# Six norm applications of the joined feed-forward and projection stage: from VectorE to ScalarE, with a bias made by GpSimd

## The reference

```
ln(v) = (v - mean) / sqrt(var + 1e-5)
x = x + attention0(ln(x), ctx)                 # 16 heads of 16
x = x + ffn0(ln(x))                            # activations rounded to 8 bits, weights to -1, 0, 1
x = x + layer1(ln(x), ctx)                     # starts with a second norm with gains (ln1),
                                               # then causal self-attention a1 (16 heads of 32), its
                                               # feed-forward, cross-attention a2, its feed-forward
x = x + moe(ln(x))                             # 8 experts, one chosen for each token

ffn0: q = round(x * 127 / max|x|)              # "front quant", one scale for each token
      h = silu(q @ Wgate) * (q @ Wup)          # 1024 wide
      y = round(h * 127 / max|h|) @ Wdown      # "hidden quant", one scale for each token
```

## Time and profile before

| | us |
|---|---|
| median of 3 runs (range) | 1103.15 (1103.12 to 1103.85) |
| profiled execution, first to last instruction (span) | 1100.8 |
| difference, what lies around the span | 2.35 |
| PE busy | 1034.3 (94%) |
| DVE busy | 535.6 (49%) |
| ACT busy | 465.3 (42%) |
| POOL busy | 268.5 (24%) |

### The profile page before, as it was taken

One profiled execution on the slowest core, in us unless ns is written; L12 is line 12 of the kernel. 1 busy time (PEld: TensorE's weight loads), 2 busy tenths in 40 slices (PEclk: granted clock), 3 DMA queues, 4 the chain that ended last, 5 costly groups with the idle time before them and its releaser, 6 DMA issues.

```text
span 1100.8 us, 20861 instructions
## 1 busy us (share of the span) xinstructions
PE 1034.3 (94%) x8679; PEld 741.0 (67%) x8679; DVE 535.6 (49%) x1293; ACT 465.3 (42%) x715; POOL 268.5 (24%) x409
## 2 busy tenths in 40 slices
PE   7998887999989999999999999999999999999997
PEld 4655544455467777776676475667578658999996
DVE  5567789985257788741531333775332233200000
ACT  6767555675455555552222325554311231122220
POOL 3023201100023334332212110566320102322211
PEclk9999989999999999999999999999999999999999
DMA  8700000000070000000000020000710217755410
GB/s 255 90 2 1 1 1 1 1 1 0 1 153 2 2 3 2 2 1 1 1 1 0 1 96 1 2 2 2 229 39 20 96 42 275 282 190 189 161 51 1
DMA packets 55359, 60.56 MB, mean 55 GB/s; under 512 B 23603, under 2 KB 47071, under 8 KB 55266
## 3 DMA queue, kind: packets, MB, share of 16 engines
q1 hardware_dynamic: 52322, 52.93, 16.3%
q0 software_dynamic: 2944, 6.30, 1.8%
HBM read 54.76 MB, written 7.21 MB: 56 GB/s over the span
## 4 chain that ended last, share of the span: by engine, by line
PE 74%; DVE 18%; ACT 3%; issue 2%; POOL 1%; SPq 1%; DMA 0%; DVEq 0%; ACTq 0%; POOLq 0%
PE ps L1882 15%; PE ps L2182 10%; DVE small L790 9%; PE ps L2324 8%; PE ps L2337 7%; PE ps L1742 6%; PE ps L2006 3%; PE ps L1713 3%; PE ps L2257 3%; PE ps L1795 2%; PE ps L1733 2%; PE ps L1710 2%; PE ps L1651 2%; PE ps L2008 1%; PE ps L1808 1%
## 5 line engine op out<-in xcount | busy, mean ns | idle before, releaser
L790 DVE TENSOR_REDUCE small<-ps 128x4 f32<-128x1024 f32 (+2 forms) x112 | 145.4, 1334 | 96.1 <-PE ps L1713 60.0
L1882 PE MATMUL ps<-r_w,r_k 128*128 128x256 f32 x512 | 113.2, 381 | 2.5 <-ACT r_k L1552 2.5
L2182 PE MATMUL ps<-r_a,r_w 128*128 128x512 f32 x256 | 112.1, 594 | 3.1 <-ACT r_a L1385 3.1
L1882 PEld LDWEIGHTS ps<-r_w,r_k 128*128 128x128 f32 x512 | 96.4, 190 | 18.6 <-issue 4.4
L1795 PE MATMUL ps<-r_a,onesf 128*32 128x256 f32 (+1 forms) x768 | 84.3, 387 | 8.3 <-ACT r_a L1305 8.3
L2182 PEld LDWEIGHTS ps<-r_a,r_w 128*128 128x128 f32 x256 | 48.2, 190 | 60.2 <-issue 56.0
L2324 PE MATMUL ps<-r_a,w_block 128*128 128x128 f32 x736 | 86.4, 275 | 1.0 <-ACT r_a L1613 1.0
L2324 PEld LDWEIGHTS ps<-r_a,w_block 128*128 128x128 f32 x736 | 85.6, 192 | 2.5 <-ACT r_a L1613 1.0
L1552 ACT ACTIVATE r_k<-ps,pvec 128x512 f32<-128x512 f32 x64 | 44.0, 687 | 100.6 <-PE ps L2182 100.6
L1305 ACT ACTIVATE r_a<-ps 120x1024 f32<-120x1024 f32 (+1 forms) x64 | 65.5, 1024 | 43.4 <-PE ps L1749 43.2
L2337 PE MATMUL ps<-w_all,r_a 128*128 x368 | 83.2, 379 | 0.2 <-issue 0.2
(11 more groups left out here) (265 smaller groups left out, 1819.9 us busy)
## 6 DMA issues: line engine op xcount, KB each, us to landing
w_block<-in_L_ffn_W SPq DMA_DIRECT2D x23, 1024.0 KB, 5.9
w_all<-in_L_ffn_W SPq DMA_DIRECT2D x8, 1024.0 KB, 9.5
r_w<-in_L_xattn_a_li_w SPq DMA_DIRECT2D x4, 1024.0 KB, 7.4
x_rows<-x_all SPq DMA_DIRECT2D x4, 512.0 KB, 3.0
x_rows<-r_a SPq DMA_DIRECT2D x4, 512.0 KB, 3.0
x_all<-in_x SPq DMA_DIRECT2D x3, 512.0 KB, 5.9
y_all<-in_L_ffn_w_gate SPq DMA_DIRECT2D x1, 1024.0 KB, 8.7
y_all<-in_L_ffn_w_up SPq DMA_DIRECT2D x1, 1024.0 KB, 11.1
```

The source lines that it names most:

```text
L790: ins_ = dve.tensor_reduce(nm.rearrange("p (j s) -> p j s", j=4)[:, j:j + count, :], src, AX.X, ALU.max, negate=True)
L1882: ins_ = pe.matmul(o[:, t // 2, (t % 2) * D:(t % 2 + 1) * D], src[:, c, t * P:(t + 1) * P], w[:, c, :], start=(c == 0), stop=(c == chunks ...
L2182: ins_ = pe.matmul(o, LI[a]["li2"][:, c, m * P:(m + 1) * P], FT3[:, c, :], start=(c == 0), stop=(c == KC - 1))
```

## The change

GpSimd's `rstd` gets a form `shift=True`: after the power it multiplies the means with the result and subtracts that from zero, so that `small` holds the bias -mean * rstd as well; only then is `rstd_ready` raised. Six of the norms of the stage use it: f of pairs 1, 2, 3 and n of pairs 0, 1, 2. Their application leaves VectorE's stream and enters ScalarE's, as four Identity activations with scale rstd and that bias. f of pair 0 and n of pair 3 stay as they were. VectorE waits for the new semaphore `xhb_ready` ahead of `front_scales(1)`, `(2)` and `(3)`. On ScalarE the six stand here (the order of all else is kept):

- `front_apply(1)` behind `silu(0,0,1)`, ahead of `weights_copy(2)`;
- `second_norm(0)` behind `whole_copy(1,0)`, ahead of `silu(1,2,1)`; `front_apply(2)` behind that `silu`, ahead of `silu(1,3,0)`;
- `front_apply(3)` behind `silu(2,0,1)`, ahead of `whole(1,3)` and `project_copy(0,3)`;
- `second_norm(1)` behind `whole_copy(2,1)`, ahead of `project_copy(0,7)`;
- `second_norm(2)` behind `project_copy(1,8)`, ahead of `whole_copy(3,1)` and `project_copy(1,9)`.

```diff
@@ GpSimd
-                def rstd(tiles=PT_TILES, twice=False):
+                def rstd(tiles=PT_TILES, twice=False, shift=False):
...
+                    if shift:
+                        link(pool.tensor_tensor(sa(at + 72, tiles), ve, neghalf[:, 0:tiles], ALU.pow))
+                        mean = sa(at + 48, 2 * tiles).rearrange("p (t k) -> p t k", k=2)[:, :, 0]
+                        link(pool.tensor_tensor(sa(at + SHIFT, tiles), mean, sa(at + 72, tiles), ALU.mult))
+                        pool.tensor_tensor(sa(at + SHIFT, tiles), zeros[:, 0:tiles], sa(at + SHIFT, tiles), ALU.subtract
+                                           ).then_inc(sem["rstd_ready"], 1)
@@ VectorE
                 gated(0, 0, 0)
-                front_apply(1, kf1)
                 gated(0, 0, 1)
+                dve.wait_ge(sem["xhb_ready"], 1)
                 front_scales(1)
...
                 attended_sum(3)
-                second_norm(0, kn0)
                 gated(1, 2, 1)
-                front_apply(2, kf2)
                 hidden_quant(1, 1)
...
                 gated(2, 0, 1)
-                front_apply(3, kf3)
                 hidden_quant(2, 0)
...
                 hidden_quant(2, 2)
-                second_norm(1, kn1)
                 down_sum(2, 0)
+                dve.wait_ge(sem["xhb_ready"], 3)
...
                 kn2 = normed_stats(2)
-                second_norm(2, kn2)
                 gated(3, 2, 1)
@@ ScalarE
+                def shifted(dst, src, k):
+                    act.wait_ge(sem["rstd_ready"], k + 1)
+                    at = LN_W * (k % 4)
+                    for t in range(PT_TILES):
+                        ins_ = act.activation(dst[:, t, :], src[:, t, :], ACT.Identity, bias=sa(at + SHIFT + t, 1), scale=sa(at + 72 + t, 1))
+                    return ins_
+
+                def front_apply(p, k):
+                    act.wait_ge(sem["n1_ready"], p)
+                    shifted(XHB, X[p], k).then_inc(sem["xhb_ready"], 1)
+
+                def second_norm(p, k):
+                    shifted(XHC, Y[p], k).then_inc(sem["c_xh_ready"], 1)
```

More of the change, by code:

```diff
@@ L67, in build @@
         epst = sb("epst", [P, 8]); neghalf = sb("neghalf", [P, 8])
-        onepe = sb("onepe", [P, 4]); eps2 = sb("eps2", [P, 4])
+        zeros = sb("zeros", [P, 4]); onepe = sb("onepe", [P, 4]); eps2 = sb("eps2", [P, 4])
         eidx = sb("eidx", [P, E])
@@ L216, in build @@
         CTX_STATS, CTX_APPLY = (16, 17, 18, 19), (21, 22, 23, 24)
-        LN_W = 80
+        LN_W, SHIFT = 80, 24
         NMX, RS, AM, SC, SU, SGT, SUT, SD = 320, 336, 352, 356, 360, 364, 372, 380
@@ L306, in build @@
                  "li1_done", "xb_ready", "yb_ready", "xh3_ready", "x3T_done", "ft3_ready", "xhq_ready", "xqT_done", "ftq_ready",
-                 "r_done", "r_ready", "dn_done", "y_ready", "cxh_ready", "cyT_done", "cyT_ready", "d_lid_ready",
+                 "r_done", "r_ready", "dn_done", "y_ready", "cxh_ready", "cyT_done", "cyT_ready", "d_lid_ready", "xhb_ready",
                  "x5_last_stored", "x5h_last_stored", "x5_half", "chosen", "x5_ready", "dn_half", "xh_half", "xT_half", "fq_half", "logits_done", "lg_ready", "x_pre_ready"]
@@ L491, in rstd @@
                         link(pool.tensor_tensor(ve, v, epst[:, 0:tiles], ALU.add))
-                    pool.tensor_tensor(sa(at + 72, tiles), ve, neghalf[:, 0:tiles], ALU.pow).then_inc(sem["rstd_ready"], 1)
+                    if shift:
[4 more added lines that the diff above has]
+                                           ).then_inc(sem["rstd_ready"], 1)
+                    else:
+                        pool.tensor_tensor(sa(at + 72, tiles), ve, neghalf[:, 0:tiles], ALU.pow).then_inc(sem["rstd_ready"], 1)
                 pool.memset(small[:], 0.0)
@@ L499, in _ @@
                 pool.memset(onepe[:], 1.0 + EPS)
+                pool.memset(zeros[:], 0.0)
                 pool.memset(eps2[:], EPS * EPS)
@@ L558, in _ @@
                         pool.tensor_tensor(X[p], X[p], bv("L0_xattn_bo"), ALU.add).then_inc(sem["xbo_ready"], 1)
-                rstd()
-                rstd()
+                rstd(shift=True)
+                rstd(shift=True)
                 rstd(twice=True)
-                rstd()
-                rstd()
+                rstd(shift=True)
+                rstd(shift=True)
                 rstd(twice=True)
-                rstd()
+                rstd(shift=True)
                 rstd(twice=True)
-                rstd()
+                rstd(shift=True)
                 rstd(twice=True)
@@ L992, in _ @@
                 hidden_quant(1, 2)
+                dve.wait_ge(sem["xhb_ready"], 2)
                 front_scales(2)
@@ L1394, in a1_input @@
                                 ).then_inc(sem[f"c_ft{e}_ready"], 1)
+                NORM_OF = {n: NP + 2 + i for i, n in enumerate(("f1", "f2", "o0", "n0", "f3", "o1", "n1", "o2", "n2"))}
+                def shifted(dst, src, k):
[9 more added lines that the diff above has]
+                    shifted(XHC, Y[p], k).then_inc(sem["c_xh_ready"], 1)
                 def project_copy(p, k):
@@ L1407, in _ @@
                 silu(0, 0, 1)
+                front_apply(1, NORM_OF["f1"])
                 weights_copy(2)
@@ L1430, in _ @@
                 whole_copy(1, 0)
+                second_norm(0, NORM_OF["n0"])
                 silu(1, 2, 1)
+                front_apply(2, NORM_OF["f2"])
                 silu(1, 3, 0)
@@ L1445, in _ @@
                 silu(2, 0, 1)
+                front_apply(3, NORM_OF["f3"])
                 whole(1, 3)
@@ L1459, in _ @@
                 whole_copy(2, 1)
+                second_norm(1, NORM_OF["n1"])
                 project_copy(0, 7)
@@ L1491, in _ @@
                 project_copy(1, 8)
+                second_norm(2, NORM_OF["n2"])
                 whole_copy(3, 1)
```

## The result

| | before | after |
|---|---|---|
| median, us (range, runs) | 1103.13 (1102.46 to 1103.85, 4) | 1123.6 (1122.23 to 1123.98, 4) |
| ratio (95% interval) | | 1.0182 (1.017 to 1.0195) |
| span of the profiled execution, us | 1100.8 | 1122.0 |

What follows compares the result with a forecast made beforehand. VectorE leads from 130 to 183 us, VectorE and TensorE are both full to 226, TensorE leads to 271. Onto 1103.15 us the places add 14.65 and the clock 2.35, together 17.0: 1120.2 us, 8-in-10 range 1109.5 to 1125.

Steps and rivals of the forecast that it cites:

- f of pair 1: ScalarE's weight copies, needed by VectorE's gated and TensorE's output(2), start at 142.82 instead of 141.43: +1.3 us.
- n of pair 0 and f of pair 2: ScalarE's a1_input copies end at 188.1, so TensorE's project(0,0) starts there for 186.05: +2.1 us.
- f of pair 3: TensorE's hidden_transposes(1,3), behind whole(1,3), starts 5.57 us late, 3.7 us of it standing still: +3.45 us on top.
- n of pair 1, standing still: TensorE's project(0,9) needs project_copy(0,7), which stands behind this norm on ScalarE: 6.6 us standstill, +6.65 us.
- given back behind it: After the project(0,9) standstill VectorE is early, so TensorE's idle 0.84 us at 224.50 goes: -0.55 us.
- n of pair 2: TensorE's project(1,11) moves +2.8 us behind project_copy(1,9); project(2,0) starts at 261.83 for 260.17: +1.7 us.
- clock, both falls: TensorE slower behind gaps: one full 1.5 us fall after the 6.6 us standstill, half after 3.7 us: +2.35 us.
- The ScalarE price: Four 128x256 activations with scale and bias from tiles take 1.93 us; six sets 11.6 us (7.5 to 16.7).
- The GpSimd tail: Product and subtraction after GpSimd's power cost 0.56 us; norm ready 1.93 us after the statistics end, before 1.4.
- A: Rival: each norm is done before ScalarE's next item is ready, so VectorE's relief pays: 1097.6 us, chance 0.05.
- B: Rival: offsets between the six places overlap instead of adding: slower, 1105.4 to 1112 us, chance 0.12.
- C: Rival: TensorE's clock falls after every new gap, 6.0 us instead of 2.35: 1123.8 us, chance 0.15.

Runs made afterwards that it cites:

- Experiment 4: Kernel before with GpSimd's added product and subtraction for the six norms, VectorE still applying them and ScalarE unchanged: 1105.37 us, ratio 1.0023.
- Experiment 3: Kernel after with unused matmuls on TensorE, 15 ahead of hidden_transposes(1,3) and 30 ahead of project(0,9): 1119.73 us, ratio 1.0143.
- experiment 9: Kernel before with only f of pairs 2 and 3 on ScalarE, placed where its stream idles: 1103.57 us, ratio 1.0003.
- experiment 6: Kernel before with only n of pair 1 on ScalarE, at the change's place: 1113.02 us, ratio 1.0087.
- experiment 7: Kernel before with only f of pairs 1 to 3 on ScalarE, at the change's places: 1110.14 us, ratio 1.0068.
- experiment 8: Kernel before with only n of pairs 0 and 2 on ScalarE, at the change's places: 1107.33 us, ratio 1.004.
- experiment 1: Kernel after with n of pair 1 back on VectorE, the other five norms staying on ScalarE: 1114.95 us, ratio 1.01.
- experiment 5: Kernel after with plain copies, without scale or bias, in place of the 24 activations: 1118.21 us, ratio 1.0133.
- experiment 2: Kernel after with n of pair 1 later on ScalarE, ahead of whole(2,2) instead of project_copy(0,7): 1115.69 us, ratio 1.0118.

## Why the prediction was right

The direction and the mechanism came out as written, and TensorE lost time at each of the places that the prediction names; the size of the first was right, the others were too small, and what was to be given back too large. The measured 1123.6 lies in the range from 1109.5 to 1125, but over the band of 1112 to 1122.5 to which I had given 0.60. Each term as TensorE's offset between the two profiles shows it:

| step | forecast, us | measured, us |
|---|---|---|
| start of the stage, before any norm | 0 | 0.4 |
| f of pair 1 | 1.3 | 1.3 |
| n of pair 0 and f of pair 2 | 2.1 | 2.35 |
| f of pair 3 | 3.45 | 3.6 |
| n of pair 1, standing still | 6.65 | 7.5 |
| given back behind it | -0.55 | -0.4 |
| n of pair 2 | 1.7 | 2.0 |
| clock, both falls | 2.35 | 3.4 |
| DMA wait at 941 us | 0 | 0.9 |
| sum | 17.0 | 21.1 (21.2 by the spans) |

The lines on the start and on the DMA wait are no effects of the change; without them the profile shows 19.8 us. The forecast for the clock has a small slip: one fall of 1.5 us and a half one make 2.3, and 2.35 was carried.

**The ScalarE price.** I took 1.93 us for a set; it is 2.06 to 2.08, each activation 583 to 600 ns. Six sets put 0.8 us on the sum. This is the term where I set the nearer row, which is 240 columns wide, above the better price. By the figures of the Trainium skill (ScalarE: Activation LUTs, What ACT_TABLE_LOAD costs) the estimates were 585 ns and 2.06 us a set, and the rows agree with the set to 0.02 us.

**The GpSimd tail.** 0.56 us was right five times of six (0.20 us each, 0.08 between). At n of pair 1 the last subtraction took 0.73 us, so the norm was ready half a microsecond later than I had it, at the place where every bit is paid. That is the main part of 7.5 for 6.65. Experiment 4 shows that at n of pair 2 the tail is paid even when VectorE applies the norm.

**The clock.** The step that was mis-sized most. I counted one fall of 1.5 us behind the long gap and half of one behind the short. Both fell in full: 3.56 us for 1.89 at the first (1.4 us net), and 7.51 for 5.4 at the second (2.0 us), where the rows show 0.50 up to 234 us and 0.74 in the two microseconds behind. Experiment 3 filled both gaps and took 3.9 us off. With two falls of 1.7 in the sum the forecast would have been 1121.2.

**What would show it.** Four of the seven signs are there as promised: 3.71 us before `hidden_transposes(1,3)`; 2.67 us at `project(1,11)`; ScalarE idle on GpSimd before f of pair 3 and n of pairs 0, 1 and 2; the clock at 0.50 behind the longest gap. Two are there in another size: the 24 activations take 0.59 us each for 0.55, and the gap before `project(0,9)` is 7.30 us for 6 to 7. The last was off: VectorE is busy 7.0 us less, not 8.3. Its groups of normalizing instructions did lose 8.2 us (28.5 to 20.3); the rest of the difference isn't in any one group.

**The rivals.** A, VectorE's relief pays: no place of the change has it, and experiment 9, with two norms that hold nothing up, shows none either. B, overlap: its 1105.4 to 1112 is out by the result, and experiments 6 to 8 show the places adding up. C, a fall of the clock behind every gap, 1123.8: the time that came is C's, but by luck: the falls cost 3.4 us and not C's 6.0, and what is missing there is in the other terms, which were short. The clock fell behind 3.71 and 7.30 us; behind the 2.67 us gap the four matmuls took 1.98 us, full speed. In other profiles the gap at this place does bring a fall: the same four take 2.98 us in experiment 1, 3.54 in experiment 3 and, behind a gap of only 1.93 us, 3.42 in experiment 5. The Trainium skill (TensorE: Matmul & The Clock Gate, HAM oscillation), by which idle gaps put the array back at half rate each time anew, was right for the two longer gaps and in some executions for the third; it deserved more weight than I gave it.

Of the ten ranges expected of the experiments, those of 4 and 9 missed. What stays open: where the 0.2 to 0.9 us at the start of the stage come from; why the same gap brings a fall of the clock in one execution and not in another, which may also be behind the slower executions among the four of experiments 1 and 3; and whether the 1 us by which the whole is less than its parts is more than chance.

## What to carry to other kernels

A busy share says that an engine has time, not when. Before work moves to an engine with room, look up what stands behind it in that engine's stream, when its input is ready, and who waits for the next item: here one norm, ready 5.4 us after ScalarE came to it, stopped projections that never used it, and four copies further down it cost 8 us less. Where TensorE stands still for microseconds, add the slower work behind the gap to the gap itself.

## What the runs showed of the hardware

- GpSimd's 128x4 subtraction took 0.20 us at five of the six norms. At n of pair 1 it took 0.73, and ended 0.06 us after a VectorE instruction that it ran beside. The two engines' rows of the kernel after:

```profile
227.40 0.73 POOL L496 TENSOR_TENSOR small<-zeros,small 128x4 f32<-128x4 f32 x1
```

```profile
227.33 0.74 DVE L924 TENSOR_SCALAR r_a<-r_a,small 128x1024 f32<-128x1024 f32 x1
```

  The subtraction took 0.73 or 0.74 us there in every profile that has it at n of pair 1 (experiments 2 to 6), and at no other norm. The product just before it ran its 0.20 us beside two VectorE instructions of one column. The Trainium skill (SBUF — State Buffer, SBUF: two separate sides) says that the two engines share a port pair that one of them holds for a whole instruction; these rows agree.
- An activation with scale and bias from a tile took 586 to 588 ns for 256 float32 columns, a plain copy of the same 404.
- Work that is thrown away can pay: 45 unused matmuls in the kernel after saved 3.9 us by the medians, 43 in the kernel before 1.9 us. The granted clock behind the filled gaps was 1.00 for 0.50.
- A gap of TensorE of one length need not act the same each time: behind 2.66 or 2.67 us the same four matmuls took 1.98 us (the kernel after, experiments 2 and 8), 2.98 (experiment 1) or 3.54 (experiment 3).
